# Moving one GRU pass from ScalarE to VectorE, one rounding pass the other way, and rolling the GRU loops of a six-sublayer decoder kernel

## The chip, the core and the metric

The kernel runs on one core of a Trainium2 chip. The metric is the device time of one execution in microseconds (us). The engines are TensorE (PE; its weight loads are PEld), VectorE (DVE), ScalarE (ACT), GpSimd (POOL) and SyncE (SP), which issues most DMAs.

## What is computed

Two decoder layers on x of shape (8, 256, 256): batch b, 256 tokens, 256 features, float32. Each sublayer is followed by x = layernorm(x + sublayer(x)). The two that the change touches are the first and the third:

```python
# sublayer 1: a minimal GRU, one batch at a time
z = sigmoid(x @ Wz + bz);  h_tilde = x @ Wh + bh
h = scan(h_t = (1 - z) * h_(t-1) + z * h_tilde)      # over the 256 tokens
out = sigmoid(h @ Wg + bg) * h
# sublayer 3: activations quantized to whole numbers, ternary weight
xq = round(clip(xn / scale, -127, 127)) * scale
out = xq @ wq.T
```

Sublayers 2, 4 and 5 are attentions with 16 heads of 16 features (the fourth with relative positions), sublayer 6 is a gated feed-forward.

## The kernel before

Every engine has a hand-written program; the order on an engine is the order in which its Python functions are called, and engines wait for each other on semaphores. Three stages follow one another, with a barrier of all engines between them. Stage one is the GRU with the cross attention, stage two (from about 298.6 us) the relative attention with the quantized product inside it, stage three the last attention and the feed-forward.

**The GRU.** For each batch b of eight, TensorE makes four kinds of work in the order `z_product(b+1)`, `turn_xn(b-2)` (transposes of the normalised output), `h_product(b+1)`, `turn_y(b-1)`, `gate_product(b)`. ScalarE makes th = tanh of half of z's input (`z_tanh`, line 340), then from th two arrays: zz = 0.5 th + 0.5, which is z (`take_part`, line 347), and za = 0.5 - 0.5 th, which is 1 - z (`keep_part`, line 351); then a tanh for the gate. VectorE's iteration is: `gated_input(b)` (line 397, hb = (h + bias) * zz, two instructions), `gru_norm_end(b-2)` (line 205, xn), `gated_output(b-1)` (lines 407 and 409), `scan(b)` (line 419, two instructions), `gru_norm_begin(b-1)` (lines 187, 193, 196: statistics and ve). GpSimd makes rstd = ve to the power -1/2 (line 471) and copies xn away (line 475). `turn_xn` waits for VectorE's xn, and VectorE's statistics wait for `turn_y`. All loops over b are Python loops, so each iteration has its own instructions; constants stand in all waits.

**The quantized product in stage two.** Stage two has 8 batches of four rounds (n = 4b + j, four heads each). Batch f of the quantized product, f = 4 to 7, is spread over batch b = f - 4: in round j = 3 VectorE scales and clips (`clip`, line 2585), adds and clamps so that the value is rounded (`round_`, line 2590), and takes the added constant away again, writing bf16 (`subtract_magic`, line 2596). TensorE turns the result (`turn_whole`, line 2095) in `fourth_round`, after the transposes `turn(n, 2)` and after a wait for the ScalarE copy `copy_rel(b+2, 0)` (line 2404); then come `turn(n, 3)`, `weigh(n-1)` and the output projection. ScalarE's program of the next round starts with `turned_bands` (line 2382), and `copy_rel(b+2, 0)` is second. For f = 0 to 3, before the rounds, ScalarE makes that last step itself (`make_whole`, line 2420).

Of the kernel before, what the change touches and what calls it, by code (L numbers as in the profile page):

```python
# [95 lines left out]
def decoder_kernel(nc, xT, ctxT, fside, mask0, mask1, wmats, cols_d, rows_d, gb, gate_up, down,  # L96
                   ident_d, rel_k_d, rel_v_d, mix_d, consts_d, out):
    ctx = ExitStack()
    with ctx:
# [134 lines left out]
        def glu_weights():  # L234
# [38 lines left out]
        g_tanh, g_za, g_zz, g_hb, g_gate, g_h, g_y = (  # L273
            sem(f"gru_{n}") for n in ("tanh", "za", "zz", "hb", "gate", "h", "yT"))
        g_steps, g_stat, g_rstd, g_xn = (sem(f"gru_{n}") for n in ("steps", "stat", "rstd", "xn"))
        g_half, g_evac, g_kept = sem("gru_half"), sem("gru_evac"), sem("gru_kept")
        loaded_wz, loaded_wh, loaded_wg, loaded_x1 = (sem(f"loaded_{n}") for n in ("Wz", "Wh", "Wg", "x_second"))
# [10 lines left out]
        def h_product(pe, b):  # L288
            ge(pe, g_hb, b)
            project_cols(pe, h_bank, W["Wh"], batch(x_feat, b), gh_mm)  # L290
# [16 lines left out]
        def gru_products(pe):  # L307
# [20 lines left out]
            for b in range(2, B - 1):  # L328
# [6 lines left out]
        def z_tanh(act, b):  # L335
            act.wait_ge(gz_mm, b + 1)
            ge(act, g_zz, b)
# [6 lines left out]
        def take_part(act, b):  # L344
            act.wait_ge(g_tanh, b + 1)
            ge(act, g_hb, b)
            act.activation(zz, th[:, :, :], ACT.Identity, bias=hbias[:, 4:5], scale=0.5).then_inc(g_zz, 1)

        def keep_part(act, b):
# [16 lines left out]
        def gru_gates(act):  # L366
# [7 lines left out]
            take_part(act, 0)  # L374
            keep_part(act, 0)
            z_tanh(act, 1)
            take_part(act, 1)
# [3 lines left out]
            take_part(act, 2)  # L381
            keep_part(act, 2)
            gate_tanh(act, 1)
            for b in range(2, B - 1):
                z_tanh(act, b + 1)
                take_part(act, b + 1)
# [4 lines left out]
        def gated_input(dve, b):  # L391

            dve.wait_ge(g_zz, b + 1)
            dve.wait_ge(gh_mm, b + 1)
            ge(dve, g_h, b)
# [4 lines left out]
            last.then_inc(g_hb, 1)  # L400
# [12 lines left out]
        def scan(dve, b):  # L413

            dve.wait_ge(g_hb, b + 1)
# [25 lines left out]
        def gru_scans(dve):  # L441
# [16 lines left out]
            for b in range(2, B - 1):  # L458
                gated_input(dve, b)
                gru_norm_end(dve, b - 2)  # L460
                if b == 2:
                    dve.wait_ge(loaded_x1, 16)
                if b == 3:
                    dve.wait_ge(loaded_x, 16 * FT)
# [12 lines left out]
        def gru_inverses(pool):  # L477
# [3 lines left out]
            for b in range(B - 3):  # L481
# [121 lines left out]
        def attention_bias():  # L603
# [33 lines left out]
            with nc.Block(no_gpsimd_drain=True) as block:  # L637
# [194 lines left out]
                def _(act):  # L832
# [39 lines left out]
                    act.wait_ge(g_zz, B)  # L872
# [1052 lines left out]
        def attention_relative():  # L1925
# [83 lines left out]
            with nc.Block(no_gpsimd_drain=True) as block:  # L2009
# [348 lines left out]
                def _(act):  # L2358
# [103 lines left out]
                    for b in range(B):  # L2462
                        for j in range(NQ):
                            n = NQ * b + j
                            if n >= 3:
                                turned_bands(n - 3)
# [52 lines left out]
                def _(dve):  # L2519
# [72 lines left out]
                    def subtract_magic(f):  # L2592

                        dve.wait_ge(q_round, f + 1)
                        dve.wait_ge(qt_mm, f)
                        dve.tensor_scalar(q_tok[:, :, :], clipped(f), -MAGIC, None, ALU.add).then_inc(q_whole, 1)

# [72 lines left out]
                    for b in range(B):  # L2670
                        for j in range(NQ):
# [30 lines left out]
                            if j == 3 and b + FF_EARLY + 1 < B:  # L2702
                                clip(b + FF_EARLY + 1)
                                round_(b + FF_EARLY + 1)
                                subtract_magic(b + FF_EARLY + 1)
# [325 lines left out]
```

## Time and profile before

| | us |
|---|---|
| median of 3 runs | 927.45 |
| lowest, highest | 927.1, 928.43 |
| the profiled execution's own time | 927.1 |
| its span in the trace | 925.3 |

The profiled execution is the fastest of the three; 1.8 us of its time lie outside the span. Over the span TensorE is busy for 93%, VectorE for 74%, ScalarE for 67% and GpSimd for 45%. Timelines list instructions by start with their length; a bracket gives the idle time of that engine just before, and what ended it. Neighbouring instructions overlap by a few hundredths, so what an instruction adds to its engine's path is read from one start to the next.

### The profile page before, as it was taken

Reading aid. Unit: us, or ns where it says so; the run is one execution under the profiler, and the core shown is the slowest. Engines: PE = TensorE matmul, PEld = TensorE weight load, DVE = VectorE, ACT = ScalarE, POOL = GpSimd, SP = SyncE. Lnnn points to the kernel's source line nnn. Section 1 sums busy time; section 2 is a strip of 40 time slices with the busy share of each in tenths; the row PEclk is TensorE's granted clock in tenths of the full one; section 3 lists DMA queues with packets and bytes.
Section 4 is the critical chain, followed back from the end, with each engine's and each line's share of the span. In section 5 each row is a group of like instructions: output and inputs, shape, how many; then the busy total and the mean of one; then the engine's idle time right before and its main releaser. Section 6 shows DMA issues by size and latency. Waiting matters only on the chain. (4 is left out here: it accounts for less than half of the span.)

```text
span 925.3 us, 21117 instructions
## 1 busy us (share of the span) xinstructions
PE 861.7 (93%) x7006; PEld 621.4 (67%) x7017; DVE 681.9 (74%) x2515; ACT 620.9 (67%) x1608; POOL 413.0 (45%) x428
## 2 busy tenths in 40 slices
PE   9998989999987788999999999897999999999996
PEld 7876766777666466777777776675666666655554
DVE  4988888888877656687686676525888878866875
ACT  4548677777762367787787787735888888864441
POOL 2256246567342345434444342243455555326432
PEclk9999999999998899999999999997999999999998
DMA  9334100000005187797787788440000000000001
GB/s 327 115 113 117 42 24 24 25 24 13 13 25 204 55 279 241 226 277 219 244 251 227 242 256 253 140 165 4 27 27 28 27 28 24 2 2 1 24 24 46
DMA packets 96960, 101.89 MB, mean 110 GB/s; under 512 B 26877, under 2 KB 92157, under 8 KB 96598
## 3 DMA queue, kind: packets, MB, share of 16 engines
q1 hardware_dynamic: 96292, 100.20, 34.6%
q8 instruction: 58, 0.95, 0.4%
q14 instruction: 48, 0.39, 0.1%
q10 hardware_dynamic: 562, 0.35, 0.1%
HBM read 48.70 MB, written 51.82 MB: 109 GB/s over the span
## 5 line engine op out<-in xcount | busy, mean ns | idle before, releaser
L222 PE MATMUL bank<-x_feat,w_all_mats 128*128 128x256 f32 x384 | 94.6, 391 | 2.1 <-ACT q_full L340 0.6
L2746 POOL TENSOR_TENSOR bnd<-bnd,consts 128x60 f32<-128x60 f32 x64 | 18.1, 303 | 149.5 <-DMA bnd<-band_scratch 149.5
L222 PEld LDWEIGHTS bank<-x_feat,w_all_mats 128*128 128x128 f32 x384 | 71.0, 192 | 15.4 <-ACT rw L2404 4.3
L2364 ACT ACTIVATE bias_area<-bias_area,mq_two 128x256 f32<-128x256 f32 x128 | 66.2, 529 | 0.0
L1680 DVE COPY q_heads<-bank 128x512 f32<-128x512 f32 x64 | 42.7, 686 | 28.8 <-PE bank L1386 28.8
L1427 PE MATMUL bank<-dist,rw 128*128 128x512 bf16 x277 | 62.9, 379 | 0.7 <-issue 0.2
L845 ACT ACTIVATE q_heads<-bank 128x512 f32<-128x512 f32 x64 | 37.7, 589 | 37.9 <-PE bank L664 37.9
L2537 DVE COPY q_heads<-bank 128x512 f32<-128x512 f32 x64 | 41.4, 683 | 26.2 <-PE bank L2036 26.2
L931 DVE COPY q_heads<-bank 128x512 f32<-128x512 f32 x64 | 41.8, 683 | 25.3 <-PE bank L664 25.3
L837 ACT ACTIVATE Sx<-Sx,mq 128x256 f32<-128x256 f32 x128 | 54.4, 499 | 5.7 <-DVE mq L923 5.6
L1672 DVE CUSTOM_DVE_ANT_0 Sx<-bank,bias_area 128x256 f32<-128x256 f32 x128 | 46.5, 419 | 14.3 <-PE bank L1372 13.9
L1574 ACT ACTIVATE Sx<-Sx,mq 128x256 f32<-128x256 f32 x128 | 54.2, 499 | 3.1 <-DVE mq L1672 3.1
L1582 ACT ACTIVATE q_heads<-bank 128x512 f32<-128x512 f32 x64 | 37.6, 590 | 27.6 <-PE bank L1386 26.9
L2382 ACT ACTIVATE w_all_mats<-bank 108x512 f32<-108x512 f32 x32 | 19.0, 595 | 53.7 <-PE bank L2068 53.7
L837 ACT ACTIVATE Pr<-Pr,mq 128x256 f32<-128x256 f32 x128 | 54.3, 500 | 0.9 <-DVE mq L923 0.9
L1574 ACT ACTIVATE Pr<-Pr,mq 128x256 f32<-128x256 f32 x128 | 54.3, 502 | 0.0
L1386 PE MATMUL bank<-ident,Sx 128*128 128x128 f32 x256 | 40.1, 286 | 11.5 <-ACT q_heads L1582 8.5
L1427 PEld LDWEIGHTS bank<-dist,rw 128*128 128x128 bf16 x288 | 28.1, 98 | 31.7 <-issue 0.4
L585 POOL TENSOR_SCALAR q_par<-q_full,cols 128x512 f32<-128x512 f32 x16 | 24.9, 1565 | 52.6 <-ACT q_full L579 50.0
L923 DVE CUSTOM_DVE_ANT_0 Sx<-bank,bias_area 128x256 f32<-128x256 f32 x128 | 46.4, 418 | 2.3 <-PE bank L650 2.3
L2529 DVE CUSTOM_DVE_ANT_0 bias_area<-bank,dist 128x256 f32<-128x256 f32 x128 | 46.9, 420 | 1.4 <-DMA dist<-skew_scratch 1.4
L230 PE MATMUL bank<-w_all_mats,aT 128*128 128x256 f32 x192 | 47.3, 389 | 0.2
(275 smaller groups left out, 2494.8 us busy)
## 6 DMA issues: line engine op xcount, KB each, us to landing
dist<-skew_scratch SPq DMA_DIRECT2D x64, 296.0 KB, 4.2
skew_scratch<-rw SPq DMA_DIRECT2D x32, 588.0 KB, 4.5
bnd<-band_scratch SPq DMA_DIRECT2D x64, 108.0 KB, 2.7
band_scratch<-bias_area SPq DMA_DIRECT2D x32, 162.0 KB, 2.7
band_scratch<-bias_area SPq DMA_DIRECT2D x32, 148.0 KB, 2.5
skew_scratch<-dist SPq DMA_DIRECT2D x4, 1024.0 KB, 8.5
context_values<-dist SPq DMA_DIRECT2D x8, 512.0 KB, 2.6
v_two<-context_values SPq DMA_DIRECT2D x8, 512.0 KB, 3.5
```

Source lines behind the costliest of these rows:

```text
L222: last = pe.matmul(dst[:, m * S:(m + 1) * S], w[:, k, m * P:(m + 1) * P], rhs[:, k, :], start=(k == 0), stop=(k == FT - 1))
L230: last = pe.matmul(dst[:, t * D:(t + 1) * D], src[:, k, t * P:(t + 1) * P], w[:, k, :], start=(k == 0), stop=(k == FT - 1))
L837: last = act.activation(rows_of(g, t), rows_of(g, t), ACT.Exp, bias=mq[:, g, t:t + 1], scale=-1.0)
L923: dve.tensor_tensor_reduce(out=rows_of(g, t), in0=s_bank[g][:, t * S:(t + 1) * S], in1=bias_two[:, b % 2, t, :], scale=-1.0, scalar=3e38, ...
L931: dve.tensor_copy(PTq[:, 4 * (n % 2) + g, :, :], t_bank[g % 2][:, :].rearrange("p (k q) -> p k q", k=TT))\
L1427: last = pe.matmul(dst[:, :], w_[:, k, m * P:(m + 1) * P], x_parts[i][:, k, p * PAIR:(p + 1) * PAIR], start=(k == 0 and i == 0), stop=(k = ...
L1574: last = act.activation(rows_of(g, t), rows_of(g, t), ACT.Exp, bias=mq[:, g, t:t + 1], scale=-1.0)
L1672: dve.tensor_tensor_reduce(out=rows_of(g, t), in0=s_bank[g][:, t * S:(t + 1) * S], in1=x1_bias_two[:, b % 2, t, :], scale=-1.0, scalar=3e3 ...
L1680: dve.tensor_copy(PTq[:, 4 * (n % 2) + g, :, :], t_bank[g % 2][:, :].rearrange("p (k q) -> p k q", k=TT))\
L2364: last = act.activation(rows_of(n, g)[:, t, :], rows_of(n, g)[:, t, :], ACT.Exp, bias=mq_two[:, n % 2, g, t:t + 1], scale=-1.0, accum_out= ...
L2529: dve.tensor_tensor_reduce(out=rows_of(n, g)[:, t, :], in0=s_bank[g][:, t * S:(t + 1) * S], in1=dist_pairs[:, t, 2 * j + g // 2, :, g % 2] ...
L2537: dve.tensor_copy(PTq[:, 4 * (n % 2) + g, :, :], t_bank[g % 2][:, :].rearrange("p (k q) -> p k q", k=TT))\
```

## The change

Three things are edited.

1. zz is made by VectorE, as first step of `gated_input`, with a wait for its own result before hb; `take_part` is gone from ScalarE. One semaphore, `g_zsteps`, counts zz and hb in turn in place of two.
2. The GRU loops become hardware loops (`Fori`): TensorE 4 iterations (b = 3 to 6), ScalarE 5, VectorE 4, GpSimd 5. VectorE's and TensorE's iteration b = 2 is written out before them.
3. For f = 4 to 7 the last rounding step is ScalarE's `make_whole`, put at the head of round 4(b+1), and `subtract_magic` is gone from VectorE.

```diff
         def h_product(pe, b):
-            ge(pe, g_hb, b)
+            ge(pe, g_zsteps, 2 * b)
...
-            for b in range(2, B - 1):
+            z_product(pe, 3)
+            turn_xn(pe, 0, xT_bank)
+            h_product(pe, 3)
+            turn_y(pe, 1)
+            gate_product(pe, 2)
+            with pe.Fori(3, B - 1) as b:
...
         def z_tanh(act, b):
             act.wait_ge(gz_mm, b + 1)
-            ge(act, g_zz, b)
+            ge(act, g_zsteps, 2 * (b - 1) + 1)
...
-        def take_part(act, b):
+        def keep_part(act, b):
             act.wait_ge(g_tanh, b + 1)
-            ge(act, g_hb, b)
-            act.activation(zz, th[:, :, :], ACT.Identity, bias=hbias[:, 4:5], scale=0.5).then_inc(g_zz, 1)
-
-        def keep_part(act, b):
...
-            for b in range(2, B - 1):
+            with act.Fori(2, B - 1) as b:
                 z_tanh(act, b + 1)
-                take_part(act, b + 1)
...
         def gated_input(dve, b):
 
-            dve.wait_ge(g_zz, b + 1)
+            step = Steps(dve, g_zsteps, b, 2)
+            dve.wait_ge(g_tanh, b + 1)
+            step(dve.tensor_scalar(zz[:, :, :], th[:, :, :], 0.5, 0.5, ALU.mult, ALU.add))
+            step.wait()
             dve.wait_ge(gh_mm, b + 1)
-            ge(dve, g_h, b)
...
+            with dve.Fori(3, B - 1) as b:
                 gated_input(dve, b)
                 gru_norm_end(dve, b - 2)
...
-            for b in range(B - 3):
+            with pool.Fori(0, B - 3) as b:
                 gru_inverse(pool, b)
...
                             n = NQ * b + j
+                            if j == 0 and 1 <= b and b + FF_EARLY < B:
+                                make_whole(b + FF_EARLY)
                             if n >= 3:
                                 turned_bands(n - 3)
...
-                    def subtract_magic(f):
-
-                        dve.wait_ge(q_round, f + 1)
-                        dve.wait_ge(qt_mm, f)
-                        dve.tensor_scalar(q_tok[:, :, :], clipped(f), -MAGIC, None, ALU.add).then_inc(q_whole, 1)
...
                                 round_(b + FF_EARLY + 1)
-                                subtract_magic(b + FF_EARLY + 1)
```

How this stands on the engines, in two places. First VectorE in the GRU, from the second pass of `gated_output` to the next iteration's start. Before (k_two holds za and zz, q_full th, Sx hb and h):

```order
L409 SCALAR_TENSOR_TENSOR Pr<-Pr,x_feat 128x512
L419 SCALAR_TENSOR_TENSOR Sx<-k_two,Sx 128x256 x2
L187 BN_STATS st<-bank 128x6 x2
L193 BN_AGGR mv<-st 128x2 x2
L196 TENSOR_SCALAR ve<-mv 128x2
L397 SCALAR_TENSOR_TENSOR Sx<-bank,cols,k_two 128x256 x2
L205 TENSOR_SCALAR xn<-bank,mv,rstd 128x256 x2
```

With the change, on VectorE at the same place (lines are the changed kernel's; ISA and REGISTER_ALU compute registers):

```order
L409 SCALAR_TENSOR_TENSOR Pr<-Pr,x_feat 128x512
L415 REGISTER_ALU
L419 SCALAR_TENSOR_TENSOR Sx<-k_two,Sx 128x256 x2
L187 BN_STATS st<-bank 128x6 x2
L72 ISA
L193 BN_AGGR mv<-st 128x2 x2
L87 REGISTER_ALU
L196 TENSOR_SCALAR ve<-mv 128x2
L465 REGISTER_ALU
L465 COMPARE_AND_BRANCH
L392 TENSOR_SCALAR k_two<-q_full 128x512
L396 SCALAR_TENSOR_TENSOR Sx<-bank,cols,k_two 128x256 x2
```

The pass L392 stands between ve and hb, behind the loop's branch, and register instructions stand between the others.

Second, ScalarE in stage two, at the end of round 3 of batch 1 and the start of round 0 of batch 2. Before:

```order
L2364 ACTIVATE bias_area,den<-bias_area,mq_two 128x256 x4
L2382 ACTIVATE w_all_mats<-bank 108x512
L2404 ACTIVATE rw<-bank 128x4x80
L2373 ACTIVATE q_heads<-bank 128x512
L2427 ACTIVATE q_feat<-bank 128x512
L2364 ACTIVATE Sx,den<-Sx,mq_two 128x256 x4
```

With the change, on ScalarE at the same place:

```order
L2367 ACTIVATE bias_area,den<-bias_area,mq_two 128x256 x4
L2423 ACTIVATE q_tok<-w_all_mats,neg_magic 128x512
L2385 ACTIVATE w_all_mats<-bank 108x512
L2407 ACTIVATE rw<-bank 128x4x80
L2376 ACTIVATE q_heads<-bank 128x512
L2430 ACTIVATE q_feat<-bank 128x512
```

The pass L2423 stands ahead of `turned_bands` and of `copy_rel` (rw), for which `turn_whole` on TensorE waits; it is before them in four batches, b = 1 to 4. TensorE's own order in stage two is as it was.

## Rows read from the trace of the kernel before

**Rows 1.** The page, part 1: busy time, share of the span, instructions of each engine.
```profile
PE 861.7 (93%) x7006; PEld 621.4 (67%) x7017; DVE 681.9 (74%) x2515; ACT 620.9 (67%) x1608; POOL 413.0 (45%) x428
```

**Rows 2.** Timeline, VectorE, one GRU iteration: start us, length us, instruction.
```profile
26.15 0.87 DVE L397 SCALAR_TENSOR_TENSOR Sx<-bank,cols,k_two 128x256 f32<-128x256 f32 x2
...
27.11 0.99 DVE L205 TENSOR_SCALAR xn<-bank,mv,rstd 128x256 f32<-128x256 f32 x2
28.02 0.68 DVE L407 SCALAR_TENSOR_TENSOR Pr<-Pr,Sx 128x512 f32<-128x512 f32 x1
...
28.74 0.98 DVE L409 SCALAR_TENSOR_TENSOR Pr<-Pr,x_feat 128x512 f32<-128x512 f32 x1
...
29.64 1.26 DVE L419 TENSOR_TENSOR_SCAN Sx<-k_two,Sx 128x256 f32<-128x256 f32 x2
...
31.18 0.76 DVE L187 BATCH_NORM_STATS2 st<-bank 128x6 f32<-128x256 f32 x2 [0.28 <-PE bank L214]
...
32.33 0.17 DVE L196 TENSOR_SCALAR ve<-mv 128x2 f32<-128x2 f32 x1
32.45 0.88 DVE L397 SCALAR_TENSOR_TENSOR Sx<-bank,cols,k_two 128x256 f32<-128x256 f32 x2
```

**Rows 3.** Timeline, TensorE, the same iteration.
```profile
28.38 0.60 PE L214 MATMUL bank<-ident,xn 128*128 128x128 f32 x4
...
30.54 0.60 PE L214 MATMUL bank<-ident,Pr 128*128 128x128 f32 x4
```

**Rows 4.** Timeline, VectorE, the gated input of batches 2 and 7.
```profile
20.03 0.88 DVE L397 SCALAR_TENSOR_TENSOR Sx<-bank,cols,k_two 128x256 f32<-128x256 f32 x2
...
51.60 0.87 DVE L397 SCALAR_TENSOR_TENSOR Sx<-bank,cols,k_two 128x256 f32<-128x256 f32 x2
```

**Rows 5.** Groups by line and form (xcount, busy, mean ns); then line 2420, min/median/max ns.
```profile
L2590 DVE TENSOR_SCALAR w_all_mats<-w_all_mats 128x512 f32<-128x512 f32 x5 | 4.1, 812 | 0.2
...
L2596 DVE TENSOR_SCALAR q_tok<-w_all_mats 128x512 bf16<-128x512 f32 x4 | 3.4, 844 | 0.1
...
L2590 DVE TENSOR_SCALAR Sx<-Sx 128x512 f32<-128x512 f32 x2 | 0.9, 428 | 0.1
...
L2420 ACT ACTIVATE q_tok<-w_all_mats,neg_magic x1: 712/712/712, 321.6 to 321.6; 128x512 bf16<-128x512 f32 x1
```

**Rows 6.** Timeline, second stage, batch 1, end of round 3.
```profile
393.17 0.79 DVE L2596 TENSOR_SCALAR q_tok<-w_all_mats 128x512 bf16<-128x512 f32 x1
...
394.57 0.59 ACT L2382 ACTIVATE w_all_mats<-bank 108x512 f32<-108x512 f32 x1
...
395.05 0.43 ACT L2404 ACTIVATE rw<-bank 128x320 f32<-128x320 f32 x1
...
395.53 0.23 PEld L2095 LDWEIGHTS bank<-ident_bf,q_tok 128*128 128x128 bf16 x4 [0.30 <-ACT rw L2404]
...
399.49 0.69 DVE L181 TENSOR_TENSOR y_sb<-bank,x_tok 128x512 f32<-128x512 f32 x1 [1.58 <-PE bank L230]
```

**Rows 7.** Timeline, second stage, the same place in batches 2 and 3.
```profile
430.98 0.23 PEld L2095 LDWEIGHTS bank<-ident_bf,q_tok 128*128 128x128 bf16 x4 [0.72 <-ACT rw L2404]
...
466.45 0.23 PEld L2095 LDWEIGHTS bank<-ident_bf,q_tok 128*128 128x128 bf16 x4 [0.70 <-ACT rw L2404]
```

**Rows 8.** Timeline, second stage, the same place in batch 0.
```profile
355.35 2.12 POOL L2735 COPY rw<-rw 128x856 f32<-128x856 f32 x2
...
357.59 0.59 ACT L2382 ACTIVATE w_all_mats<-bank 108x512 f32<-108x512 f32 x1
...
360.21 0.44 ACT L2404 ACTIVATE rw<-bank 128x320 f32<-128x320 f32 x1 [2.03 <-DMA skew_scratch<-rw]
```

**Rows 9.** DMA queue of code; TensorE records up to 26.6 us; longest wait behind a branch.
```profile
q8 instruction: 58, 0.95, 0.4%
...
0.00:26.60 26.60, 24.65 (x116) 21.33 (x117) 14.71 (x41) 12.36 (x22) 5.64 (x8) 1.00 0.96 330
...
PE bank L222 <- PEq L2938: 1.7, 1, 1.7
```

## What the change does to the time, predicted from the trace of the kernel before

> **What bounds the kernel now.** I read the page's busy times first. TensorE is busy for 93% of the span and the other engines for 45 to 74% [rows 1], but that is a mean over stages, so it says only that TensorE is often last. What counts is which wait ends last at the two places of the change, and that is in the timelines.
>
> In the GRU one iteration on VectorE is a row of instructions with hardly a gap: hb at 26.15, xn at 27.11, the two passes of the output at 28.02 and 28.74, the scan at 29.64, statistics at 31.18, ve at 32.33, next hb at 32.45 [rows 2]. That is 6.30 us, and the only wait is 0.28 us before the statistics, for TensorE's transposes. The wait is part of a loop through both engines: xn on VectorE releases `turn_xn`, behind it come `h_product` and `turn_y` on TensorE, and only then VectorE's statistics. On TensorE that piece lasts from 28.38 to 30.54 + 0.60 = 31.14, 2.76 us [rows 3]. So two paths are nearly equally long. The path through both engines is hb to xn 0.96, xn 0.99, TensorE 2.76, statistics to the next hb 1.27, and about 0.1 for the two handovers: 6.08. VectorE alone, with its 0.28 wait taken out, is 6.02. The mean from batch 2 to batch 7 is (51.60 - 20.03) / 5 = 6.31 [rows 4]. Each path runs through ve and hb, which is where the change puts a pass.
>
> In stage two TensorE transposes the quantized batch (`turn_whole`). At 395.53 it had been idle for 0.30 us, and the rw copy of ScalarE released it; that copy stands second in ScalarE's row of 394.57, 395.05 [rows 6]. In the next two batches the same wait is 0.72 and 0.70 us, with the same releaser [rows 7]. VectorE's `subtract_magic` had ended at 393.96, 1.6 us earlier [rows 6]: it is not what TensorE waits for. In the first of the four batches ScalarE itself waits 2.03 us for a DMA before the rw copy at 360.21 [rows 8].
>
> **The change part by part.**
>
> zz on VectorE: eight passes of 128x512 float32 from SBUF to SBUF with two constants. `round_` has that very form and lasts 0.428 us where GpSimd is quiet, and 0.812 us on average where it streams [rows 5]. In the GRU GpSimd's only work at that moment is the power of two numbers a partition, so I take 0.43. It is followed by a wait for its own result; between the two output passes, which wait in the same way, start to start is 0.72 for an instruction of 0.68 [rows 2], so 0.04 more: 0.47 us. The passes of batches 0 and 1 lie in gaps at the start, and cost nothing: there zz takes the place of a ScalarE pass for which VectorE waited, and TensorE is behind with `h_product`. If that cover were gone they would cost 0.47 each. The six of batches 2 to 7 stand on both paths above. The path through TensorE becomes 6.08 + 0.47 = 6.55 and VectorE alone 6.49, so the period goes from 6.30 to 6.55 in an iteration like this one, and by the full 0.47 where VectorE did not wait. That is 0.25 to 0.47 an iteration; I take 0.4, since more than half of it is unsheltered, and 6 x 0.4 = 2.4 us. The bounds are 1.5 and, at 0.812 us a pass, 6 x 0.85 = 5.1.
>
> ScalarE loses its 8 passes. Nothing follows from it: its za pass waits for the scan and its tanhs for products of TensorE, as before, so it only waits longer for the same events.
>
> The loops: VectorE gets 4 iterations, so a branch behind ve and in front of zz, four times, and some register instructions, of which the one before the second output pass comes behind a wait. No row shows a branch alone. One bound is 0; the other is the longest TensorE wait behind a stage's branch, 1.7 us [rows 9], which also holds a barrier of five engines and the reset of semaphores. I take 0.3 us an iteration, close to the lower end, because the barrier is the larger part of that row: 4 x 0.3 = 1.2 us, between 0 and 6.8. The loops on ScalarE and GpSimd are covered by their waits, and the one on TensorE by the time for which it will now wait for xn: xn comes 0.47 later, and TensorE took it up 0.28 late, 28.10 to 28.38 [rows 2, 3], which leaves 0.2 in such an iteration and more in one without that lateness, 0.3 on average. Without that cover it would cost as much as VectorE's. The Trainium skill, "Advanced Engine Details and Errata", section Control Flow Timing, gives 51 ns for a branch and 108 ns for a compare-and-branch. By it this term would be about 0.6 us, an estimate from that page's figures; no run here shows them.
>
> The rounding step in stage two: VectorE loses 4 passes of 0.79 to 1.0 us, 0.844 on average [rows 5]. Behind them VectorE's copies start earlier, but TensorE's next step is still held by the rw copy. ScalarE gains 4 passes of 0.712 us [rows 5]. They stand ahead of `turned_bands` and rw. ScalarE's instructions overlap: 394.57 to 395.05 is 0.48 for a length of 0.59 [rows 6], so a pass adds 0.60. In batches 1, 2 and 3 ScalarE has no gap at this place and TensorE already waits for rw, so `turn_whole` and all behind it, up to the projection whose result VectorE awaits at 399.49 for 1.58 us [rows 6], come 0.60 later: 3 x 0.60 = 1.8 us, between 0 and 3 x 0.72. In the first batch the pass fits into the 2.03 us of waiting [rows 8], and costs 0; if GpSimd's fill before that DMA, 2.12 us for two [rows 8], is quicker without VectorE beside it, 0.1 or 0.2 us come back. `load_affine` on SP waits for the moved step too, but it is issued a round later.
>
> Sum: 2.4 + 1.2 + 1.8 = 5.4 us. The profiled execution took 927.1, which gives 932.5; the median of the runs is 0.35 above it, so 932.9.
>
> **The rivals.**
>
> *The order of code.* TensorE's loop body could lie across a border of the blocks in which its code is loaded. The code queue moved 0.95 MB in 58 packets, 16.4 KB each; 7006 + 7017 records and some hundreds of waits make that 64 bytes an instruction, 256 a packet [rows 1, 9]. Up to 26.6 us, where its loop would begin, TensorE has 116 + 117 records [rows 9], with some ten waits 245 instructions, and the body has about 75. So the body would cross the 256th, and each of three jumps back could wait for code: at most 1.7 us, less the 0.3 of waiting, 3 x 1.4 = 4.2 more: 937.1. Against it: nothing shows that a block is dropped once it is passed. The Trainium skill, "Runtime: NRT & Kernel Launch", section Instruction fetch mechanics, has the rule: a taken branch whose target is outside the current two pages stalls for a DMA. It also gives TensorE a larger instruction memory than the others. No run here shows either.
>
> *Stage two swallows the delay.* ScalarE's pass is later made up by something on TensorE's way that is not moved, a DMA of bands for instance. Then that term is 0: 931.1. For it: in the first batch it is just such a DMA that ends last [rows 8]. Against: in the other three the rw copy starts right behind its neighbour, so the DMA is long in by then [rows 6].
>
> *GpSimd slows zz.* At 0.812 us a pass the GRU term is 6 x 0.8 = 4.8 and the time 935.3. `round_` shows that this happens beside a streaming GpSimd instruction [rows 5]; here its instruction is tiny.
>
> *Not slower.* TensorE's transposes at the end of round 3 are in truth held by VectorE, through its copies behind `subtract_magic`, and the ScalarE pass finds room. The point that decides is which of the two, VectorE's copy or the rw copy, is ready last before `turn_whole`. Then stage two gains 4 x 0.84 = 3.4 us, against 3.6 in the GRU: 927.6, and somewhat under the old time if the loops are free (926.4). Against it stand the three waits with rw as releaser [rows 6, 7].
>
> **How the numbers follow.** Forecast 0.55, order of code 0.12, swallowed 0.13, slow zz 0.08, not slower 0.12. A measurement of this kernel can tell about 0.2%, 1.9 us. Only the last case lies under 929.3; I give 0.05 of it to faster and 0.07 to the same, and one more hundredth to the same for small terms all at their low ends. That leaves 0.87 for slower. The range runs from 929.0 (GRU 1.5, no loop cost, hardly a delay in stage two) to 938.5 (code order, or loops at 1.2 us an iteration, on top of the forecast), and leaves out most of the last rival and the far end of the second.
>
> **What would show it.** In the GRU of the changed kernel, hb to hb on VectorE should be 6.5 to 6.9 us, with a pass of 0.43 us between ve and hb, and a gap of up to 0.4 us on TensorE ahead of `turn_xn`. A gap of over a microsecond on TensorE at the loop's end, three times, would be the order of code. In stage two the wait before `turn_whole` should grow by 0.60 us in batches 1 to 3 (to 0.9, 1.3 and 1.3), with rw still as releaser, and not in batch 0; stage two as a whole should be 1.8 us longer, and stage three the same. The prediction is wrong if zz lies in a gap, if `turn_whole` is no later, or if a branch costs microseconds.

## The result, and the profile after

The changed kernel took 931.45 us in the median of 18 runs, the kernel before 927.28 in 18 runs beside it. The ratio is 1.0058, with a 95% interval of 1.0044 to 1.0072, so the change costs about 5.4 us (4.1 to 6.7; the two medians are 4.2 apart). The forecast was 932.9 us and slower, with a range of 929.0 to 938.5.

The profiled execution of the changed kernel took 928.61 us, with a span of 926.8 against 925.3. That is only 1.5 us more, and a reader who stops there misses most of the change. Where the other 4 us are, the traces say; the section on why the prediction was right comes back to it. The busy times answer to [rows 1]: VectorE hardly differs, since zz added to it what the rounding step took away, and ScalarE, which loses eight passes and gains four, is busy for 2.8 us less.

```profile
PE 858.8 (93%) x7006; PEld 618.4 (67%) x7017; DVE 681.1 (73%) x2519; ACT 618.1 (67%) x1604; POOL 413.5 (45%) x428
```

One loop iteration of the GRU on VectorE, in the timeline after (start, length, instruction), answers to [rows 2]:

```profile
33.82 0.17 DVE L196 TENSOR_SCALAR ve<-mv 128x2 f32<-128x2 f32 x1
34.33 0.43 DVE L392 TENSOR_SCALAR k_two<-q_full 128x512 f32<-128x512 f32 x1 [0.35 <-issue]
34.79 0.88 DVE L396 SCALAR_TENSOR_TENSOR Sx<-bank,cols,k_two 128x256 f32<-128x256 f32 x2
...
38.11 1.26 DVE L419 TENSOR_TENSOR_SCAN Sx<-k_two,Sx 128x256 f32<-128x256 f32 x2
39.56 0.76 DVE L187 BATCH_NORM_STATS2 st<-bank 128x6 f32<-128x256 f32 x2 [0.19 <-PE bank L214]
...
41.20 0.43 DVE L392 TENSOR_SCALAR k_two<-q_full 128x512 f32<-128x512 f32 x1 [0.32 <-issue]
41.66 0.48 DVE L396 SCALAR_TENSOR_TENSOR Sx<-bank,cols,k_two 128x256 f32<-128x256 f32 x1
```

The period from hb to hb is 6.87 us (34.79 to 41.66) where it was 6.30. The zz pass takes 0.43, as forecast. New is the idle time in front of it that nothing releases ("issue"): from ve to zz it is 0.51 us start to start. That is the jump back of the loop. At the statistics (39.56) VectorE still waits for TensorE: from the scan to them it is 1.45.

TensorE in the same iteration, against [rows 3]:

```profile
36.70 0.65 PE L214 MATMUL bank<-ident,xn 128*128 128x128 f32 x4 [0.45 <-DVE xn L205]
...
38.92 0.60 PE L214 MATMUL bank<-ident,Pr 128*128 128x128 f32 x4
39.42 1.99 PE L222 MATMUL bank<-Sx,w_all_mats 128*128 128x256 f32 x8
41.26 1.89 PE L222 MATMUL bank<-x_feat,w_all_mats 128*128 x8
```

It now waits 0.45 us for xn, and there is no gap at its own jump: the last product of one iteration (39.42) and the first of the next (41.26) are 1.84 us apart, which is what eight such matmuls take.

In the second stage `turn_whole` waits for the rw copy, in batches 1, 2 and 3. The first two rows are ScalarE's in batch 1, the others TensorE's; they answer to [rows 6, 7]:

```profile
396.71 0.74 ACT L2423 ACTIVATE q_tok<-w_all_mats,neg_magic 128x512 bf16<-128x512 f32 x1
...
397.80 0.45 ACT L2407 ACTIVATE rw<-bank 128x320 f32<-128x320 f32 x1
...
398.31 0.40 PE L2098 MATMUL bank<-ident_bf,q_tok 128*128 128x128 bf16 x4 [1.24 <-ACT rw L2407]
...
434.38 0.40 PE L2098 MATMUL bank<-ident_bf,q_tok 128*128 128x128 bf16 x4 [1.15 <-ACT rw L2407]
...
470.46 0.40 PE L2098 MATMUL bank<-ident_bf,q_tok 128*128 128x128 bf16 x4 [1.13 <-ACT rw L2407]
```

From batch 1 to batch 2 it is 36.07 us now (398.31 to 434.38), where it was 35.45 (395.53 to 430.98 in [rows 6, 7]), and from 2 to 3 it is 36.08 where it was 35.47: 0.62 and 0.61 more.

### The profile page after: what moved, and what is told of

It is laid out like the page before. It is cut to its first block and busy times, and to the rows that moved or that the text cites. A ratio compares the mean times of both kernels' runs of the same rounds, so it can differ in the third digit from the quotient of the medians.

```text
span 926.8 us, 21248 instructions
## 1 busy us (share of the span) xinstructions
PE 858.8 (93%) x7006; PEld 618.4 (67%) x7017; DVE 681.1 (73%) x2519; ACT 618.1 (67%) x1604; POOL 413.5 (45%) x428
## 5 line engine op out<-in xcount | busy, mean ns | idle before, releaser
L222 PE MATMUL bank<-x_feat,w_all_mats 128*128 128x256 f32 (+1 forms) x384 | 95.4, 394 | 2.2 <-ACT q_full L345 0.6
```

The lines of the kernel that those rows point to most:

```text
L222: last = pe.matmul(dst[:, m * S:(m + 1) * S], w[:, k, m * P:(m + 1) * P], rhs[:, k, :], start=(k == 0), stop=(k == FT - 1))
```

## Experiments

The runs of one kernel spread over some 4 to 11 us, so an effect of 1 us doesn't show in a ratio. In the trace it does: the two lengths below are the same to 0.05 us in all traces whose edit doesn't touch them. Other stretches are not, and the sections behind name some. So each experiment is read twice, as a ratio and as the length of a stretch. Two lengths serve for all. The **GRU** is measured from the first output pass of batch 0 (line 407, at 15.82 us before and 16.78 after, which leaves out how late the first loads landed) to the first K copy behind the GRU (57.91 and 61.58): 42.09 us before, 44.80 after. A **batch of stage two** is measured from one residual sum of VectorE (line 181) to the next. The times before and after of the sums of batches 1, 2 and 3 are 399.49, 434.97, 470.44 and 402.27, 438.37, 474.45.

| kernel | GRU, us | against before | batches 1 to 2 and 2 to 3, us |
|---|---|---|---|
| before | 42.09 | | 35.48, 35.47 |
| changed | 44.80 | +2.71 | 36.10, 36.08 |
| zz alone on VectorE | 43.21 | +1.12 | 35.52, 35.48 |
| loops alone | 42.91 | +0.82 | 35.48, 35.48 |
| rounding step alone | 42.07 | -0.02 | 36.08, 36.07 |
| changed, VectorE written out | 43.40 | +1.31 | 36.08, 36.08 |

**zz alone.** The GRU written out, zz on VectorE, stage two as before:

```diff
-            act.activation(zz, th[:, :, :], ACT.Identity, bias=hbias[:, 4:5], scale=0.5).then_inc(g_zz, 1)
+            step = Steps(dve, g_zsteps, b, 2)
+            dve.wait_ge(g_tanh, b + 1)
+            step(dve.tensor_scalar(zz[:, :, :], th[:, :, :], 0.5, 0.5, ALU.mult, ALU.add))
+            step.wait()
```

> The kernel before with the zz pass alone moved to VectorE; the GRU is written out without loops and the rounding step of stage two stays where it was. My theory: the period from hb to hb on VectorE goes from 6.30 us to 6.5 or 6.55 and the whole costs 2.4 us (929.7 where the kernel before takes 927.3), between 1.5 and 2.8. Rival, loops alone: the pass lies in slack that TensorE's round trip leaves, the period stays at 6.3, and the time is within 1 us of before. Rival, slow zz beside GpSimd: a pass of 0.8 us and 4.8 us in all.

Measured: ratio 1.0008 (0.9982 to 1.0035), and 1.12 us more in the GRU, so less than my 1.5 to 2.8 and a little more than the 1 us of the first rival. VectorE's timeline of one iteration:

```profile
32.65 0.17 DVE L196 TENSOR_SCALAR ve<-mv 128x2 f32<-128x2 f32 x1
32.73 0.42 DVE L392 TENSOR_SCALAR k_two<-q_full 128x512 f32<-128x512 f32 x1
33.18 0.88 DVE L396 SCALAR_TENSOR_TENSOR Sx<-bank,cols,k_two 128x256 f32<-128x256 f32 x2
33.98 0.99 DVE L205 TENSOR_SCALAR xn<-bank,mv,rstd 128x256 f32<-128x256 f32 x2
...
36.50 1.26 DVE L419 TENSOR_TENSOR_SCAN Sx<-k_two,Sx 128x256 f32<-128x256 f32 x2
37.88 0.76 DVE L187 BATCH_NORM_STATS2 st<-bank 128x6 f32<-128x256 f32 x2
...
39.56 0.88 DVE L396 SCALAR_TENSOR_TENSOR Sx<-bank,cols,k_two 128x256 f32<-128x256 f32 x2
```

The period is 6.38 us, not 6.55. The pass adds 0.41 between ve and hb (0.12 before, 0.53 now), but two places became shorter. From hb to xn it is 0.80 instead of 0.96, and from the scan to the statistics 1.38 instead of 1.54 [rows 2]. The second is the wait for TensorE of 0.28, which was worth only 0.16, and stood in every other iteration only: the periods before are 6.12, 6.30, 6.14 and 6.29. The first is not marked as a wait in the rows. In the kernel before, GpSimd's power in the iteration of [rows 2] is this row of its timeline:

```profile
26.28 0.69 POOL L471 TENSOR_TENSOR rstd<-ve,neghalf 128x2 f32<-128x2 f32 x1 [3.25 <-DVE ve L196]
```

It ended at 26.97, and xn began at 27.11; hb alone would have let it begin 0.16 earlier. So it seemed that xn had waited for GpSimd, and that zz slid into that wait. The next two kernels test it.

**The zz pass twice**, the second writing the same values, in the kernel with zz alone:

```diff
             step(dve.tensor_scalar(zz[:, :, :], th[:, :, :], 0.5, 0.5, ALU.mult, ALU.add))
             step.wait()
+            step(dve.tensor_scalar(zz[:, :, :], th[:, :, :], 0.5, 0.5, ALU.mult, ALU.add))
+            step.wait()
```

> The kernel with zz alone on VectorE, and the pass made twice in every batch (the second writes the same values, with its own wait). My theory now: the first pass cost only 0.24 us or less an iteration because it fell partly into two waits, 0.17 us for GpSimd's power ahead of xn and 0.28 us for TensorE ahead of the statistics; with both used up (period 6.38 without a wait) the second pass has no cover and the period goes to 6.38 + 0.47 = 6.85 us, five periods 2.3 us longer than with one pass. Rival, VectorE is not the bound and TensorE's round trip sets 6.38: the period grows by less than 0.3 us.

Measured, in 8 runs: 1.0031 (1.0012 to 1.0050). The four periods from batch 2 to batch 6 are 6.83 to 6.85 us. The second pass costs its whole 0.46, so VectorE's own row is the bound once both waits are used up.

**GpSimd's power twice**, in the kernel before:

```diff
+            pool.tensor_tensor(spare[:, :], ve[:, :], neghalf[:, :], ALU.pow)
             pool.tensor_tensor(rstd[:, :], ve[:, :], neghalf[:, :], ALU.pow).then_inc(g_rstd, 1)
```

> The kernel before, with GpSimd's power of two numbers a partition made twice in each batch of the GRU (the first into a spare tile). My theory: xn on VectorE waited in the kernel before for that power: it ended at 26.97 and xn began at 27.11, 0.17 us later than it could have. So with a second power of 0.69 us the time from hb to xn goes from 0.96 to about 1.6 us at every batch from 2 on, and the period from 6.12 to 6.30 up to 6.7 to 6.95. Rival, xn waited for nothing but hb: the time from hb to xn goes to 1.47 at most (0.17 less of slack than I think, 0.96 + 0.69 - 0.17) or, if GpSimd ended early, stays at 0.96.

Measured, in one execution: hb in batch 3 starts at 26.87 and xn at 28.49, so 1.62 us, as my theory had it; the periods are 6.76 to 6.79. VectorE's rows:

```profile
26.75 0.17 DVE L196 TENSOR_SCALAR ve<-mv 128x2 f32<-128x2 f32 x1
...
28.49 0.99 DVE L205 TENSOR_SCALAR xn<-bank,mv,rstd 128x256 f32<-128x256 f32 x2 [0.74 <-POOL rstd L473]
```

A second power of 0.66 us moved xn by 0.66. So there was no slack between the first one's end and xn: the power stood in VectorE's row in the kernel before, and the rows [rows 2] carried no mark of it.

**Loops alone.** The kernel before with the loops of the changed one, zz on ScalarE:

```diff
-            for b in range(2, B - 1):
+            with dve.Fori(3, B - 1) as b:
...
-            for b in range(2, B - 1):
+            with act.Fori(2, B - 1) as b:
```

> The kernel before with the GRU's batches 3 to 6 in loops on TensorE, ScalarE, VectorE and GpSimd (ScalarE from batch 2, GpSimd from batch 0); zz stays on ScalarE, and stage two stays as it was. In the trace of the changed kernel the time from ve to the next zz on VectorE was 0.07 us without a branch, 0.21 at the loop's entry and 0.49 to 0.51 at its three jumps back. My theory: these 0.14 + 3 x 0.42 = 1.4 us, and 0.1 an iteration for the register instruction behind the wait, stand on the path here too, less what the wait of 0.28 us before the statistics gives up: 1 to 1.8 us in all. Rival: without zz on VectorE the waiting of VectorE swallows most of it, under 0.7 us. Rival, order of code on TensorE: over 3 us, with gaps of a microsecond on TensorE at the jumps.

Measured: ratio 1.0004 (0.9977 to 1.0031), 0.82 us more in the GRU. VectorE's jump back, with its idle time:

```profile
32.85 0.17 DVE L196 TENSOR_SCALAR ve<-mv 128x2 f32<-128x2 f32 x1
33.47 0.88 DVE L402 SCALAR_TENSOR_TENSOR Sx<-bank,cols,k_two 128x256 f32<-128x256 f32 x2 [0.45 <-issue]
34.27 0.98 DVE L205 TENSOR_SCALAR xn<-bank,mv,rstd 128x256 f32<-128x256 f32 x2
```

From ve to hb it is 0.62 instead of 0.12 us, 0.50 more. But hb to xn is 0.80 here too: the wait for GpSimd swallows 0.16 of it. Each of the two edits alone uses the same slack, some 0.16 us in each of five or six iterations, and so together they cost 2.71 and not 1.12 + 0.82 = 1.94. The result, 0.82, lies a little under my range and above the rival's.

**VectorE written out, the other loops kept**, in the changed kernel:

```diff
-            with dve.Fori(3, B - 1) as b:
+            for b in range(3, B - 1):
```

> The changed kernel with VectorE's GRU batches written out and the loops of TensorE, ScalarE and GpSimd kept. My theory: VectorE's jumps are the only ones on the path, so this gives back 1.4 to 1.8 us of the changed kernel's 4 to 5.4: 2.6 to 3.9 us slower than before, and the period from hb to hb falls from 6.87 to 6.5 us. Rival, the jumps of another engine (ScalarE's lies between the za pass and the next tanh, TensorE's ahead of z_product) take VectorE's place: the period stays above 6.7 and hardly anything is given back.

Measured: 1.0018 (0.9993 to 1.0043), GRU 43.40, so 1.40 less than in the changed kernel. That is the three jumps and the entry: (0.51 + 0.49 + 0.49) - 3 x 0.07 + 0.14 = 1.42. The period is 6.45 us. The loops of ScalarE, TensorE and GpSimd together cost the 0.19 that remain above zz alone (43.40 against 43.21). They show on TensorE: with its loop `turn_xn` starts 1.11 or 1.12 us behind the start of xn, with zz alone 1.04, and VectorE's statistics come 0.07 later in each of three iterations.

**The jump by itself.** Probes in the first microseconds of the kernel before, on engines that wait there for the first loads: four passes on one column written out, then five iterations of two.

```diff
+            for i in range(4):
+                one().then_inc(done, 1)
+                eng.wait_ge(done, i + 1)
+            with eng.Fori(0, 5) as i:
+                one().then_inc(done, 1)
+                eng.wait_ge(done, 5 + 2 * i)
+                one().then_inc(done, 1)
+                eng.wait_ge(done, 6 + 2 * i)
```

> The kernel before with small probes in the first microseconds, where VectorE and ScalarE wait for the first loads: four one-column passes written out, each with a wait for its own end, then a loop of five iterations with two such passes each, whose waits compare with a register; TensorE's eight warm-up products become four written out and five times two in a loop. My theory: from the last pass of an iteration to the first of the next, VectorE takes 0.4 us longer than between the two passes of one iteration, as in the changed kernel (0.42), and ScalarE much the same; and a register wait costs about 0.1 more than one with a constant. Rival, the 0.42 us belonged to the GRU's own instructions (a longer body, several waits behind the branch): the bare jump costs 0.05 to 0.16 us here. For TensorE I expect a gap under 0.3 us at its jumps, since none was seen in the GRU.

Measured, in one execution, rows of VectorE (461 to 465 are the kernel's own and the probe), of ScalarE, and of TensorE's weight loads in its warm-up loop:

```profile
1.08 0.46 DVE L465 MEMSET spare<- 128x1 f32 x4
...
2.41 0.18 DVE L465 MEMSET spare<- 128x1 f32 x2 [0.44 <-DVE spare L465]
3.01 0.18 DVE L465 MEMSET spare<- 128x1 f32 x2 [0.42 <-DVE spare L465]
...
5.91 0.44 ACT L378 ACTIVATE spare<-neghalf 128x1 f32<-128x1 f32 x2 [0.34 <-ACT spare L378]
6.67 0.44 ACT L378 ACTIVATE spare<-neghalf 128x1 f32<-128x1 f32 x2 [0.33 <-ACT spare L378]
...
5.02 0.30 PEld L315 LDWEIGHTS bank<-ones_w 128*128 128x128 f32 x2
5.24 0.30 PEld L316 LDWEIGHTS bank<-ones_w 128*128 128x128 f32 x2
5.46 0.30 PEld L315 LDWEIGHTS bank<-ones_w 128*128 128x128 f32 x2
```

On VectorE two passes of one iteration start 0.18 - 0.06 = 0.12 us apart (0.059 is the length of one), and an iteration takes 0.60. So the jump takes 0.60 - 0.12 = 0.48 from start to start, 0.36 more than no jump, with 0.42 of idle time. On ScalarE the pair is 0.24 apart and the iteration 0.76: 0.52, so 0.28 more. On TensorE a jump (5.24 to 5.46) takes no longer than the step inside the body (5.02 to 5.24). ScalarE's jump is cheaper than the 0.4 that I expected. And one expectation failed: a wait against a register is no slower here than one against a constant, 0.12 against (0.46 - 0.06) / 3 = 0.13.

**The rounding step alone**, the GRU as before:

```diff
+                            if j == 0 and 1 <= b and b + FF_EARLY < B:
+                                make_whole(b + FF_EARLY)
                             if n >= 3:
                                 turned_bands(n - 3)
...
-                                subtract_magic(b + FF_EARLY + 1)
```

> The kernel before with only the rounding step of stage two moved from VectorE to ScalarE for batches 4 to 7; the GRU stays as it was. My theory: turn_whole comes later by 0.60 to 0.71 us in batches 1, 2 and 3 and not in batch 0, and all behind it with it: 1.8 us in all (929.1 against 927.3), 1.4 to 2.1. Rival, swallowed: a wait behind turn_whole shrinks by as much and the time is within 0.5 us of before. Rival, VectorE held turn_whole: the time falls by up to 3.4 us.

Measured: 1.0018 (0.9995 to 1.0041), and each of the two batches of stage two 0.60 longer (table). In TensorE's list of waits (us in all, times, longest) the rw copy is the releaser four times, for 6.0 us in all:

```profile
PE bank L2095 <- ACT rw L2404: 6.0, 4, 2.6
```

In the kernel before it is three times, 3.6 us. The rival that VectorE held `turn_whole` is out.

**ScalarE's pass twice**, in that kernel:

```diff
+                        if f > FF_EARLY:
+                            act.activation(q_tok[:, :, :], clipped(f), ACT.Identity, bias=neg_magic[:, 0:1],
+                                           scale=1.0).then_inc(extra_pass, 1)
+                            act.wait_ge(extra_pass, f - FF_EARLY)
```

> The kernel with the rounding step alone moved, and ScalarE's pass made twice for batches 4 to 7, with its own wait. My theory: each further pass ahead of the rw copy moves turn_whole by its full 0.7 us (0.60 of issue and the wait for its own end) in batches 1, 2 and 3, so that one batch of stage two after the other starts 1.3 us later than in the kernel before, and batch 0 still pays nothing, since 2 us of waiting for the band DMA stand there. Rival, the 0.6 us of the first pass came from beside it (VectorE's copies in other places): the second adds less than 0.3 a batch.

Measured, in 4 runs: 1.0084 (1.0058 to 1.0110), 7.8 us where I expected some 4. From batch 1 to 2 it is 36.85 us, 1.37 more than before, as expected; from 2 to 3 it is 38.50, another 1.65. TensorE's timeline behind `turn_whole` in batches 1 and 2, then the windows with its granted clock (the third number from the end is the clock as a share of 2.4 GHz) behind batches 1 and 2; behind batch 3 (472 to 479) it is 0.76 again:

```profile
396.90 0.40 PE L2096 MATMUL bank<-ident_bf,q_tok 128*128 128x128 bf16 x4 [1.99 <-ACT rw L2405]
...
397.76 1.70 PE L2054 MATMUL bank<-q_heads,v_two 128*32 128x256 f32 x16
399.39 3.01 PE L230 MATMUL bank<-w_all_mats,aT 128*128 128x256 f32 x8
...
435.36 0.40 PE L2096 MATMUL bank<-ident_bf,q_tok 128*128 128x128 bf16 x4 [1.89 <-ACT rw L2405]
...
437.22 1.99 PE L230 MATMUL bank<-w_all_mats,aT 128*128 128x256 f32 x8
...
396.00:403.00 7.00, 6.10 (x44) 4.10 (x48) 1.55 (x9) 6.48 (x22) 2.83 (x5) 0.76 1.01 310
431.00:439.00 8.00, 6.11 (x50) 4.72 (x49) 4.08 (x19) 7.97 (x25) 4.31 (x6) 1.00 0.86 247
```

The waits of TensorE have grown to 1.9 and 2.0 us. After two of the three it ran at the lower clock for some microseconds: in batch 1 the weighted sums took 1.70 instead of 1.07 and the eight matmuls of the projection 3.01 instead of 1.99, which makes 1.65 in all. That is the further 1.65 of batch 3, too. My theory had the pass right and left the clock out: twice 1.65 and three times 1.37 are 7.4 us.

**The transposes ahead of the wait.** TensorE does head group 3's transposes before it waits for rw, in the kernel before and in the changed one:

```diff
                             turn(n, 2)
+                            turn(n, 3)
+                        if b == 0:
+                            weigh(n - 1)
                         if b + FF_EARLY + 1 < B:
                             pe.wait_ge(r_sb, 4 * (b + 2) + 1)
                             turn_whole(b + FF_EARLY + 1)
-                        if b < B:
-                            turn(n, 3)
+                        if 0 < b < B:
                             weigh(n - 1)
```

> The kernel before with TensorE's order in the fourth round changed: the transposes of head group 3 stand ahead of the wait for the rw copy and turn_whole, and in batch 0 the weighted sums of round 2 too. My theory: rw is what TensorE waits for there, 0.24 to 0.5 us in batches 1 to 3 and 2.5 us in batch 0, and 0.63 us of transposes (1.6 us with the weighted sums) can be done meanwhile: 0.3, 0.5, 0.5 and up to 1.6 us, 1.3 to 2.9 us faster in all. Rival, what follows turn_whole (the copy of it by ScalarE, ahead of the projection) becomes the wait, since only 1.0 us of work is left behind it: within 0.5 us of before.

> The changed kernel with the same new order on TensorE. My theory: waits of 1.24, 1.15 and 1.13 us for rw in batches 1 to 3 shrink by the 0.63 us of the transposes, and that of batch 0 by up to 1.6: 1.9 to 3.5 us faster than the changed kernel, so 0.7 to 3.5 us slower than before. Rival, the copy of the turned batch takes the place of the wait: as slow as the changed kernel.

Measured: on the kernel before 1.0025 (1.0008 to 1.0042), so slower and not faster; on the changed one, in 7 runs, 1.0054 (1.0035 to 1.0073), as slow as the changed kernel. The batches of the first are 35.38 and 35.34 us, 0.12 shorter instead of 0.5; those of the second 35.93 and 35.94, 0.15 shorter, with waits for rw of 0.64 to 0.67. The first row is TensorE's in batch 0 of the first, the others are from its batch 1:

```profile
367.29 3.68 PE L230 MATMUL bank<-w_all_mats,x_feat 128*128 128x256 f32 x8 [1.70 <-ACT x_feat L2434]
...
397.12 1.31 PE L2036 MATMUL bank<-ident,bias_area 128*128 128x128 f32 x8 [0.51 <-DVE q_heads L2539]
398.27 0.39 PE L2095 MATMUL bank<-ident_bf,q_tok 128*128 128x128 bf16 x4
...
404.41 2.00 PE L230 MATMUL bank<-w_all_mats,x_feat 128*128 128x256 f32 x8 [0.21 <-ACT x_feat L2434]
```

In the first, the wait for rw is gone, and in its place stands one for VectorE's copies behind its rounding step, and later one for ScalarE's copy into x_feat. The rival held, though not with the copy that I had named. In batch 0 the product behind x_feat ran at the lower clock: 3.68 us in the first kernel and 3.29 in the second, both with the new order, where the kernel before took 1.99 after a like wait of 1.59. That is where the 1.6 us expected in batch 0 went in these two traces. Whether the new order brings the lower clock on is not shown.

**The table of tanh early**, in the kernel before: one more instruction on ScalarE ahead of its first wait.

```diff
+            act.wait_ge(const_made, 3)
+            act.activation(spare[:, 0:1], neghalf[:, 0:1], ACT.Tanh)
             act.wait_ge(g_half, 1)
```

> The kernel before with one more instruction on ScalarE, a tanh of one column ahead of the wait for the biases, so that the table of tanh (1.28 us, from 7.14 to 8.42 on the way to the first tanh) is loaded while ScalarE waits for the first product. My theory: the first tanh starts at 7.6 instead of 8.44 and the GRU ends 0.6 to 0.85 us earlier; 926.5 where the kernel before takes 927.3. Rival: the product of TensorE or the load of the second batch's columns sets the start of batch 1, and nothing is gained.

Measured: 0.9998 (0.9982 to 1.0014). In the trace the first tanh starts at 7.72 instead of 8.44, and the GRU ends at 57.19 instead of 57.91: 0.72 us, within what I expected and below what the runs can tell.

**rw ahead of the bands**, with the early table: ScalarE copies rw before `turned_bands`.

```diff
-                            if n >= 3:
-                                turned_bands(n - 3)
                             if j == 0 and 1 <= b < B - 1:
                                 copy_rel(b + 1, 0)
+                            if n >= 3:
+                                turned_bands(n - 3)
```

> The kernel before with the early tanh table of the last experiment, and in stage two with ScalarE's rw copy ahead of turned_bands at the head of the rounds 4 (b + 1). It takes the 0.48 us of turned_bands out of the way to rw, as the change put 0.60 in. My theory: turn_whole waits for rw in batches 2 and 3 by 0.7 us and in batch 1 by 0.3, so stage two ends 0.48 us earlier in each of 2 and 3 and 0.2 to 0.3 in 1 (batch 0 waits for a DMA and gains nothing): 1.2 us, and 0.72 with the table, 1.9 in all. Rival, VectorE's copies or the later turned_bands take the place of the wait: only the 0.72 remain.

Measured: 1.0008 (0.9992 to 1.0024), no gain. The batches are 35.30 and 35.29 us, 0.18 shorter each and not 0.48. In the list of what TensorE's matmuls wait for, one of the four waits for rw is left (the weight loads still wait for it by 0.26 and 0.25 in batches 2 and 3, where it was 0.72 and 0.70). This is the list's line, and TensorE's weight loads later in batch 1:

```profile
PE bank L2098 <- ACT rw L2407: 2.6, 1, 2.6
...
402.40 0.73 PEld L230 LDWEIGHTS bank<-w_all_mats,x_feat 128*128 128x128 f32 x4 [0.24 <-ACT x_feat L2435]
```

Most of the time that `turn_whole` gained is waited for again 6 us later, ahead of a product with ScalarE's copy into x_feat. ScalarE has no gap from 391.5 to that copy. So behind the one wait stands ScalarE's whole row: what is added to the row comes out in full (0.60), and what is only moved within it comes out in part. Neither this version nor the early table beats the kernel before by more than the runs can tell.

## Why the prediction was right, and which terms were mis-sized

**Direction and total** were right: 5.4 us were forecast, 5.4 (4.1 to 6.7) measured. The terms are less good than their sum. That the sum agrees so well is luck: zz was priced 1.3 us too high, the loops 0.4 too low, and 0.85 came from a place that no term had.

**zz on VectorE, forecast 2.4 us, measured 1.12.** The step that failed is the path through both engines. I added up hb to xn 0.96 as work, and put the pass on top of it in full. In it lay 0.16 of waiting for GpSimd. With zz the period is VectorE's own row, 6.38. The value for the pass itself, 0.47, was right, as the doubled pass showed (0.46). So VectorE's own work without zz is 6.38 - 0.46 = 5.92, where I had 6.02.

The sum also left out TensorE's own row. My two paths came to 6.08 and 6.02, and neither explains a period of 6.30, which was moreover one of the long ones. In the kernel before TensorE's matmuls show a single wait, of 0.4 us, between 19 and 52 us, and one round of its three products and two sets of transposes takes 6.14:

```profile
26.65 1.89 PE L222 MATMUL bank<-x_feat,w_all_mats 128*128 128x256 f32 x8
...
32.79 1.89 PE L222 MATMUL bank<-x_feat,w_all_mats 128*128 128x256 f32 x8
```

VectorE's row with the power in it is 6.12 (6.78 with the second power, less its 0.66). The periods of 6.12 to 6.30 lie at these two or a little above. zz had to fill the distance from 5.92 up to there before it cost anything, and then cost 0.26 or 0.08 a period and not 0.4.

**The loops, forecast 1.2, measured 2.71 - 1.12 = 1.59** on top of zz, of which VectorE's 1.40. A jump back took 0.42, three times, and the entry 0.14, where I took 0.3 four times. That the other engines' loops are covered held to 0.19. The Trainium skill, "Advanced Engine Details and Errata", section Control Flow Timing, gives 51 ns for a branch and 108 ns for a compare-and-branch. By that the term was about 0.6, an estimate from these figures; the probe shows 0.36 a jump on VectorE and 0.28 on ScalarE, so the figures do not cover a loop's jump as these engines see it. The measurement decides.

**The order of code** did not happen at the jumps. TensorE's loop body has no gap at its jump, three times, and the probe's TensorE loop has none. The Trainium skill, "Runtime: NRT & Kernel Launch", section Instruction fetch mechanics, says that a taken branch to a target outside the current two pages stalls for a DMA. No such stall shows here; whether this body crosses such a border isn't known, so the rule itself is left open.

**The rounding step, forecast 1.8, measured 0.64, 0.63 and 0.61** in the places for batches 1, 2 and 3: from the K copy of batch 1 at 372.99 to that of batch 4 at 478.87 the changed kernel's delay grows from 2.13 to 4.01, 1.88 in all. The forecast of the waits, 0.9, 1.3 and 1.3, was made from rows of weight loads; the same rows have 1.43, 1.34 and 1.32 now. In batch 1 the wait grew by more than the pass, because the transposes ahead of it came earlier, at 396.44 where 394.71 + 2.13 = 396.84 was due: with `subtract_magic` gone VectorE's copies start at 395.18 where 393.88 + 2.13 = 396.01 was due. So much of the rival *not slower* was true, but rw is still last. The mechanism, the rw copy as releaser, was right but too narrow, since taking rw out of the way gains little.

**Batch 0, forecast 0, held** in the pair of traces: from the K copy of batch 0 (338.28, and 340.39 in the changed kernel) to that of batch 1 the delay goes from 2.11 to 2.13. ScalarE still waits 1.23 us for the store of rw with the pass in front. How late that store lands differs between traces: behind the K copy of batch 0 the rw copy starts at 21.93 us before, 21.73 in the changed kernel and with the rounding step alone, 20.79 with zz alone, and 22.54 in the changed kernel with VectorE written out. So a small effect of the pass can't be excluded, but none shows.

**The last batch, no term of mine.** In the three kernels in which VectorE's GRU is a loop, a batch late in stage two is longer: between the sums of VectorE (line 181) at 543.33 and 576.89 the changed kernel took 33.56 us, the loops alone 33.95, the changed kernel with the transposes ahead 33.65. The eleven others took 32.68 to 32.71, VectorE written out among them. In those three VectorE waits 0.77 to 1.00 us for a DMA at a place where the others have no wait, and 1.7 to 1.9 us behind the first of the two sums the queue of code loads a block, which it does in none of the others within 1 to 3 us. The changed kernel's row, and the queue in its window from 544.7 to 545.8:

```profile
547.82 0.42 DVE L2534 CUSTOM_DVE_ANT_0 bias_area<-bank,dist 128x256 f32<-128x256 f32 x1 [0.77 <-DMA dist<-skew_scratch]
...
q8 instruction: 1, 0.02, 5.5%
```

So a loop in the GRU may well cost 0.85 us here, almost 500 us later, by moving a load of code into the way of a transfer. That is argued from fourteen traces; no kernel moves the load alone. With it the terms give 2.71 + 1.88 + 0.85 = 5.44, without it 4.6, and both lie in the interval.

**The profiled span grew by 1.5 us only**, because the two executions differ in their clock. At 118.60 the profiled execution of before ran eight matmuls in 3.02 us that took 1.89 in that of the changed kernel. The windows of before, then of the changed kernel:

```profile
116.00:124.00 8.00, 6.31 (x39) 5.02 (x40) 6.43 (x29) 4.29 (x11) 3.69 (x4) 0.79 0.22 66
626.00:644.00 18.00, 12.73 (x93) 8.90 (x96) 10.21 (x47) 9.74 (x23) 6.39 (x5) 0.72 0.02 5
```

```profile
116.00:124.00 8.00, 5.79 (x56) 4.13 (x56) 7.97 (x33) 4.19 (x10) 3.46 (x4) 1.00 0.22 68
626.00:644.00 18.00, 12.71 (x89) 8.68 (x89) 8.26 (x36) 9.70 (x24) 9.18 (x8) 0.81 0.02 4
```

The delay of the changed kernel falls from 3.69 to 2.13 us between 112 and 142, from 4.85 to 2.92 between 572 and 604, and from 2.92 to 1.49 between 621 and 676. At the first place the kernels with zz alone, loops alone and the rounding step alone differ from before by the same 1.55. So it is before's execution that was slow there, not the change that was fast. The account closes: 0.96 for the first loads, which landed later, 2.71, 1.88 and 0.85, less 1.56, 1.93 and 1.43, make the 1.5 of the spans.

## What to carry to other kernels

A distance between two starts on an engine is not all work, even where no wait is marked: compare it with the same pair elsewhere, or with the length of the instructions, before an added pass is put on top of it. A loop's jump back costs 0.3 to 0.5 us on VectorE and ScalarE, at each of its turns, wherever the engine has no wait at that point to cover it. And where an engine's row has no gap, taking away the wait that it causes downstream mostly moves the wait to its next product. A total that agrees to 0.1 us says nothing of its terms: measure each in its own stretch.

## What the runs showed of the hardware

A jump back took 0.36 us (probe), 0.42 (changed kernel) and up to 0.50 (loops alone) more than no jump on VectorE, 0.28 on ScalarE and nothing on TensorE, whose matmuls followed one another without a gap. Two edits that each used the same slack of 0.16 us cost 1.12 and 0.82 alone and 2.71 together. A load of a block of code and a transfer that landed 0.77 to 1.00 us too late fell together in the three traces with VectorE's loop and in none of the eleven others.

TensorE's clock made differences of 1 to 2 us that don't belong to any kernel. After idle times of 2 us it ran at the lower of its two levels (1.2 GHz) for some microseconds in one batch and at the upper (2.4 GHz) after a like wait in the next: 3.01 and 1.99 us for the same eight matmuls. Before the slow stretch at 118 it had waited 2.21 us for ScalarE; in the changed kernel the same wait of 2.21 us came at 121.37, and the clock stayed up. Behind a wait of 2.58 us for rw in batch 0 the clock stayed up in the changed kernel and fell with the rounding step alone, where sixteen matmuls then took 1.94 us instead of 1.07. So the length of a stretch behind such a wait is worth comparing only where both traces show the same clock.
